# One step sequence for layer 0's row maxima, found half a pair ahead, with other slots for the third steps

## The chip, the cores and the metric

The kernel runs on one core of a Trainium2 chip. The metric is the device time of one execution in microseconds (us), smaller is better. Before the change it is 1639.65 us, the median of three executions (1639.27 to 1640.0 us). The engines are TensorE (PE in the profile), VectorE (DVE), ScalarE (ACT), GpSimd (POOL) and SyncE (SP), which issues the loads. Each runs its own list of instructions in order and waits for the others by semaphores.

## The reference, cut to what matters

The program is a two-layer decoder over 1024 tokens of width 128 and a context of 6404 rows of width 96. The change touches the cross attention of layer 0, and what is laid beside its last part. The cross attention has 8 heads of 64, which the kernel works in 4 pairs:

```python
q = (x @ Wq).reshape(B, Nq, HEADS, DIM_HEAD)
k = (context @ Wk).reshape(B, context.shape[1], HEADS, DIM_HEAD)
v = (context @ Wv).reshape(B, context.shape[1], HEADS, DIM_HEAD)
sim = jnp.einsum('bihd,bjhd->bhij', q, k) * SCALE
attn = jax.nn.softmax(sim, axis=-1)
out = jnp.einsum('bhij,bjhd->bihd', attn, v)
```

The softmax needs a shift near each row's largest score. Layer 1 later rounds the context to integers (`jnp.round(x / i_scale)`), projects it, and needs the largest magnitudes for the scales; the kernel begins that in the last pair of layer 0.

## The kernel before

A pair of heads is worked in two halves of 512 queries (`hf` counts them, 0 to 7). In a half the 51 key tiles of 128 rows go by in 26 units of two tiles, and each unit is a *slot*: 52 slots for each pair, `s` from 0 to 51. Nothing is scheduled at run time. Each engine has the same loop over pairs and slots, and the lists written out in `ITEMS` and the step tables say what stands in each slot.

In a slot TensorE computes the scores of the unit's two tiles (L2153, 6 pairs of matmuls), and the values of the unit before (L2167, 4 pairs, fp32). The two heads lie on 64 rows each, so two matmuls run side by side. ScalarE takes the exponential of each tile (L933), 128x1024. VectorE (L1432) adds three quarters of it to a running sum, and GpSimd (L708) the last quarter (`dve_part`, `SHARE`), in halves 0 to 5. In halves 6 and 7 VectorE adds all.

The row maxima are found ahead, from rounded keys and queries. The keys are folded: max(a, b) = (a + b)/2 + |a - b|/2, so the kernel makes sums and differences of keys half a context apart (`k16_in`, L2004 and L2005, called `kd` and `ks` in the tables; `k16_out` copies them to `K16`). A *step* is one tile of 128 queries of one head against one chunk of 512 differences and 512 sums: TensorE writes the difference scores into bank 6 (`x_ps`) and the sum scores of the step before into bank 7 (`y_ps`), both L2199; ScalarE writes the magnitude of bank 6 to `MC` (L959, `x_cp`); VectorE combines bank 7 with it and takes the maximum (`half_max`, L1382, `mx`). Step m on TensorE waits for ScalarE's step m-1 and VectorE's step m-2. The last chunk has 130 columns only, and takes up to three query tiles in a step.

Before the change pair 0's maxima, for all 1024 queries, are found ahead of the loop by themselves (`max_alone` over the 52 items of `ALONE0`, L2116, L912, L1382, chunks of twice the width). The maxima of pair p+1 are found inside pair p: 102 steps (`STEPS`, `NM`) in its slots 2 to 50, two in a slot, and a third one in slots 32, 36, 40, 44 and 48 (`THIRD_M`). In slots with a third step it lies between the score matmuls of the first and the second tile (`split_steps`). At the pair's end VectorE turns the maxima into shifts (`shifts`) and writes them on diagonals (`diagonals`), which `seeds` adds to the scores by matmuls (L2138).

Bank 5 of the PSUM serves one after the other: next pair's queries (`q`), keys (`dk`, fp32-like from three products, in the odd slots from 27), values (`v`, in the even slots from 28), denominators (`den`), output projection (`wo`). In pair 3 there are no steps, and the `CHAIN` list of layer 1 lies beside the slots: `scale`, `round` (VectorE L1570, then ScalarE L985), `project` (TensorE into banks 6 and 7, from slot 12), `max`. GpSimd finds the maximum over partitions (L716).

Of the kernel before, what the change touches and what calls it, by code (L numbers as in the profile page):

```python
# [99 lines left out]
def micro_steps(s):  # L100
    if not FIRST_M <= s <= LAST_M:
        return []
    a = 2 * (s - FIRST_M) + sum(t < s for t in THIRD_M)
    return list(range(a, a + 2 + (s in THIRD_M)))


assert micro_steps(LAST_M)[-1] == NM


def split_steps(s):  # L110
    steps = micro_steps(s)
    return steps[0:1], steps[1:-1], steps[-1:]
# [44 lines left out]
BANK_OF = {("q", 0): 6, ("q", 1): 7, ("kd", 0): 6, ("ks", 0): 7}  # L159


def bank_of(x):
    return BANK_OF.get((x[0], x[1][1]), 5) if x[0] in ("q", "kd", "ks") else 5


BANK5 = [x for p in range(PAIRS) for s in range(SLOTS) for x in ITEMS[p][s] if x[0] in FREED_BY and bank_of(x) == 5]
# [2545 lines left out]
```

## Time and profile before

| | |
|---|---|
| median of 3 executions | 1639.65 us |
| profiled execution, its own time | 1638.51 us |
| span of the profiled execution | 1636.8 us |
| TensorE busy | 1530.1 us (93% of the span) |
| VectorE busy | 1286.3 us (79%) |
| ScalarE busy | 1126.0 us (69%) |
| GpSimd busy | 490.9 us (30%) |
| granted TensorE clock, mean | 0.964 |

The busy time of an engine is the time in which at least one of its instructions shows as running. Instructions of an engine overlap at their ends, so the pace of an engine is better read from the starts of consecutive instructions than from their durations. The maxima by themselves take the span from 59.6 to about 125 us, the four pairs follow from 128.6 to about 1000 us, and 636.8 us of other work follow.

### The profile page before, as it was taken

What the parts mean: (1) busy time and instruction counts of PE and PEld (TensorE: products, weight loads), DVE (VectorE), ACT (ScalarE), POOL (GpSimd) and SP (SyncE); (2) the same over time, 40 slices, a digit from 0 to 9 for tenths busy, and PEclk for the clock granted to TensorE, in tenths of its full rate; (3) what the DMA queues carried; (4) which work ended last, traced back from release to release, by engine and by line L of the source; (5) the groups of instructions that cost most, each with busy time, mean ns of one, the idle gap of its engine ahead of it and who ended that gap; (6) DMA issues with size and microseconds to landing.
All of it is one profiled execution on the core that took longest, in us unless ns stands there. A gap on an engine that the chain in (4) does not pass through costs nothing.

```text
span 1636.8 us, 27033 instructions
## 1 busy us (share of the span) xinstructions
PE 1530.1 (93%) x9058; PEld 548.9 (34%) x9058; DVE 1286.3 (79%) x2319; ACT 1126.0 (69%) x1541; POOL 490.9 (30%) x488
## 2 busy tenths in 40 slices
PE   6889999999999999999999998899997979999986
PEld 4312333333333333333333223344444612222223
DVE  6898987879977779878789897877775666787766
ACT  6787777768877778777777786655554469676643
POOL 6303343334543334433300010345451012233100
PEclk9759999999999999999999998999999979999998
DMA  4000000000200000000010000111100000000000
GB/s 135 7 1 11 1 1 1 1 2 11 54 1 2 1 1 1 3 1 11 20 32 3 1 1 19 37 46 45 45 27 1 1 1 2 0 1 1 1 14 13
DMA packets 14834, 22.79 MB, mean 14 GB/s; under 512 B 1990, under 2 KB 11766, under 8 KB 14710
## 3 DMA queue, kind: packets, MB, share of 16 engines
q1 hardware_dynamic: 14710, 21.22, 4.6%
q8 instruction: 68, 1.11, 0.3%
q14 instruction: 56, 0.46, 0.1%
HBM read 20.69 MB, written 0.52 MB: 13 GB/s over the span
## 4 chain that ended last, share of the span: by engine, by line
PE 69%; issue 11%; DVE 9%; POOL 5%; ACT 4%; DMA 0%; POOLq 0%; SPq 0%; DVEq 0%; ACTq 0%
PE PS L2167 22%; PE PS L2153 15%; PE PS L2511 6%; PE PS L2199 5%; POOL WRK L734 5%; PE PS L2498 3%; DVE KNB L1382 3%; PE PS L2020 2%; PE PS L2012 2%; PE PS L2116 2%; PE PS L2540 2%; PE PS L2450 1%; PE PS L2435 1%; PE PS L2004 1%; ACT KNB L959 1%
## 5 line engine op out<-in xcount | busy, mean ns | idle before, releaser
L1382 DVE CUSTOM_DVE_ANT_0 KNB<-PS,KNB 128x512 f16<-128x512 f32 (+2 forms) x500 | 338.5, 690 | 152.4 <-PE PS L2199 106.9
L1432 DVE TENSOR_TENSOR WRK<-WRK 128x768 f32<-128x768 f32 (+3 forms) x400 | 425.2, 1063 | 15.3 <-ACT WRK L933 8.4
L933 ACT ACTIVATE WRK<-PS 128x1024 f32<-128x1024 f32 (+1 forms) x408 | 401.4, 1022 | 47.6 <-PE PS L2153 39.2
L2167 PE MATMUL PS<-WRK,V 128*64 128x512 f32 (+1 forms) x1632 | 395.7, 605 | 0.0
L708 POOL TENSOR_TENSOR WRK<-WRK 128x256 f32<-128x256 f32 x300 | 274.7, 916 | 395.6 <-ACT WRK L933 394.6
L959 ACT ACTIVATE KNB<-PS 128x512 f16<-128x512 f32 (+2 forms) x306 | 180.9, 591 | 77.8 <-PE PS L2199 77.2
L2344 PE MATMUL PS<-WRK,KNB 128*128 128x512 f16 x828 | 188.3, 381 | 7.1 <-POOL WRK L734 2.7
L2167 PEld LDWEIGHTS PS<-WRK,V 128*64 128x64 f32 (+1 forms) x1632 | 99.3, 136 | 192.7 <-issue 154.5
L2153 PE MATMUL PS<-KNB,KB 64*128 64x512 f16 (+1 forms) x1224 | 156.5, 377 | 0.0
L2153 PE MATMUL PS<-Q,KB 64*128 64x512 f16 (+1 forms) x1224 | 153.0, 377 | 0.0
L1162 ACT ACTIVATE WRK<-PS 128x1024 f32<-128x1024 f32 x100 | 102.4, 1024 | 51.1 <-PE PS L2498 47.6
L734 POOL TENSOR_TENSOR WRK<-KB,WRK 128x1024 f16<-128x1024 f32 x46 | 98.4, 2140 | 119.5 <-ACT WRK L1088 119.5
L2344 PEld LDWEIGHTS PS<-WRK,KNB 128*128 128x128 f16 x828 | 80.8, 98 | 106.7 <-issue 4.3
L1846 DVE TENSOR_TENSOR WRK<-WRK 128x768 f32<-128x768 f32 (+2 forms) x100 | 103.8, 1038 | 10.6 <-ACT WRK L1162 8.9
L2511 PE MATMUL PS<-WRK,V 128*64 128x512 f32 (+1 forms) x408 | 112.0, 617 | 0.0
L1624 DVE TENSOR_TENSOR KA<-PS,KB 128x1024 f32<-128x1024 f32 x46 | 56.3, 1225 | 48.3 <-PE PS L2344 48.3
L757 POOL TENSOR_TENSOR WRK<-WRK 128x256 f32<-128x256 f32 x72 | 56.2, 781 | 126.5 <-ACT WRK L1162 126.5
L2199 PE MATMUL PS<-KNB,Q 64*128 64x512 f16 (+1 forms) x448 | 79.3, 357 | 9.4 <-DVE MXP L1382 5.2
L2153 PEld LDWEIGHTS PS<-Q,KB 64*128 64x128 f16 (+1 forms) x1224 | 55.6, 94 | 88.8 <-ACT WRK L933 20.5
L2153 PEld LDWEIGHTS PS<-KNB,KB 64*128 64x128 f16 (+1 forms) x1224 | 59.6, 94 | 62.6 <-issue 12.7
L912 ACT ACTIVATE KNB<-PS 128x1024 f16<-128x1024 f32 x60 | 61.2, 1023 | 17.3 <-DVE MXP L1382 10.0
L1075 ACT ACTIVATE KB<-PS 128x1024 f32<-128x1024 f32 x46 | 47.1, 1023 | 35.0 <-PE PS L2344 35.0
(379 smaller groups left out, 1834.2 us busy)
## 6 DMA issues: line engine op xcount, KB each, us to landing
V<-in_moe_w_dram SPq DMA_DIRECT2D x44, 192.0 KB, 2.4
KNB<-in_ctx_fm_dram SPq DMA_DIRECT2D x6, 384.0 KB, 8.4
X<-in_ctx_fm_dram SPq DMA_DIRECT2D x12, 192.0 KB, 2.4
...
```

The costliest lines, as they stand in the source:

```text
L708: e.tensor_tensor(total, total, part, ALU.add).then_inc(S("acc_pool"), 1)
L734: e.tensor_tensor(H_LO[hslot], MH[hslot % 2], H_HI[hslot], ALU.subtract).then_inc(S("h_lo"), 1)
L933: e.activation(PR[0:r, u % 2, b, :], bank(2 * b, 2 * b + 2, slice(0, r)), ACT.Exp).then_inc(S("exp"), 1)
L959: e.activation(MC[:, m % 2, 0:w], PS[:, 6, 0:w], ACT.Abs).then_inc(S("x_cp"), 1)
L1382: return e.tensor_tensor_reduce(diffs, sums, diffs, 0.5, NEG, ALU.add, ALU.max, accum_out=out)
L1432: e.tensor_tensor(total, total, part, ALU.add).then_inc(S("acc"), 1)
L1846: e.tensor_tensor(total, total, part, ALU.add).then_inc(S("acc"), 1)
L2153: ins = e.matmul(PS[0:r, 2 * b + h, :], keys[rows, j * P:j * P + r], queries[rows, :], start=False, stop=(k == 2), skip_group_check=True)
L2167: ins = e.matmul(PS[h * HD:(h + 1) * HD, 4, :], V[0:r, j, h * HD:(h + 1) * HD], PR[0:r, unit_no(hf, i) % 2, b, h * HALF:(h + 1) * HALF], s ...
L2199: ins = e.matmul(PS[:, b, k * w:(k + 1) * w], QH[(p + 1) % 2][rows, t * P:(t + 1) * P], K16[rows, off + a:off + a + w], start=True, stop=True)
L2344: ins = e.matmul(bank(b + h), w_[:, part, :], rows[:, h * HALF:(h + 1) * HALF], start=start and i == 0, stop=stop and i == 2, skip_group_c ...
L2511: ins = e.matmul(PS[g * HD:(g + 1) * HD, 4, :], V2[n // 2][0:w, j, :], PR1[t % len(PR1)][0:w, g * HALF:(g + 1) * HALF], start=(i == 0), st ...
```

## The change

1. `ALONE0` has 26 items in place of 52: only the first 512 queries of pair 0 ahead of the loop.
2. `STEPS` becomes two lists of 52 steps, one for each half of queries, and all later halves (1 to 7) form one sequence of `NSTEP` = 364 steps that runs through the slots from slot 0 of pair 0 on: two in every slot, pairs' ends included, until slot 11 of pair 3.
3. Third steps: in pair 0 in slots 3, 4, 5, 23, 24, 26, 36, 40, 44, 48; in pairs 1 and 2 in slots 6, 9, 14, 16, 17, 20, 21, 23, 24, 26; none in pair 3. So 30 where there were 15.
4. `shifts` and its diagonals now come for one half at a time, seven times, at the start of the slot behind the one in which a half's last step lies: slots 25 and 49 of pair 0, 20 and 44 of pair 1, 16 and 39 of pair 2, and 12 of pair 3.
5. The sums and differences of the next pair's keys move to slots 6/7, 9/10, 13/14, 16/17, 20/21, 23/24 and 25/26. The queries move to slots 1 and 2. All of them use bank 5; before, the queries and the first chunk used banks 6 and 7, in slots 0 and 1.
6. GpSimd takes its quarter of the sums in half 6 too (`POOL_HALVES` = 7), and its three maxima over partitions lie between those sums.
7. The rounded context goes to `KA[1]` instead of `KN[0]`.

```diff
-STEPS = full_then_rest(NFULL, lambda t: (0, 1), 3)
-NM = len(STEPS)
+TILES_H = NT // 2
+STEPS = [[(c, [t], g) for c in range(NFULL) for t in range(TILES_H * u, TILES_H * u + TILES_H) for g in range(2)]
+         + [(NFULL, list(range(TILES_H * u + a, TILES_H * u + b)), g) for a, b in ((0, 3), (3, TILES_H)) for g in range(2)] for u in range(2)]
+NM = len(STEPS[0])
...
-ALONE0 = full_then_rest(NDC - 1, lambda t: (0, 1), 6)
+ALONE0 = [(d, [t], g) for d in range(NDC - 1) for t in range(TILES_H) for g in range(2)] + [(NDC - 1, [0, 1, 2, 3], g)
...
+POOL_HALVES = 2 * PAIRS - 1
...
-    return SHARE if hf < 2 * (PAIRS - 1) else T
+    return SHARE if hf < POOL_HALVES else T
...
-THIRD_M = (32, 36, 40, 44, 48)
...
+NSTEP = NM * (2 * PAIRS - 1)
+WITH_KEYS = (6, 9, 14, 16, 17, 20, 21, 23, 24, 26)
+THIRD_M = [(3, 4, 5, 23, 24, 26, 36, 40, 44, 48)] + [WITH_KEYS] * (PAIRS - 2) + [()]
+
+
+def first_step(p, s):
+    return min(2 * (p * SLOTS + s) + sum(len(x) for x in THIRD_M[:p]) + sum(t < s for t in THIRD_M[p]), NSTEP + 1)
...
+def split_steps(p, s):
+    steps = micro_steps(p, s)
+    return steps[:1], steps[1:-1], steps[1:][-1:]
...
+K16_AT = (6, 9, 13, 16, 20, 23, 25)
...
-        at[0] += [("wk", n), ("q", (n, 0)), ("q", (n, 1))]
-        at[1] += [("wv", n), ("kd", (n, 0)), ("ks", (n, 0))]
-        for c in range(1, NMC):
-            at[4 + 3 * c].append(("kd", (n, c)))
-            at[5 + 3 * c].append(("ks", (n, c)))
+        at[0].append(("wk", n))
+        at[1] += [("wv", n), ("q", (n, 0))]
+        at[2].append(("q", (n, 1)))
+        for c, k in enumerate(K16_AT):
+            at[k].append(("kd", (n, c)))
+            at[k + 1].append(("ks", (n, c)))
...
-        EMB = [KN[0].bitcast(BF16), KN[1].bitcast(BF16), KN[0].bitcast(BF16)]
+        EMB = [KA[1][:, :].bitcast(BF16), KN[1].bitcast(BF16), KN[0].bitcast(BF16)]
...
-                    if s == SLOTS - 1 and p + 1 < PAIRS:
-                        shifts(micro_base(p + 1), NMC, 2 * NT)
-                        e.wait_ge(S("sc"), tile_no(2 * p, 0, 0) + 1)
-                        diagonals(0, 2, NT)
+                    first, mid, last = split_steps(p, s)
+                    if ready(p, s):
+                        shifts(ready(p, s), STEP0 + ready(p, s) * NM, NMC)
```

How the order of instructions changes is shown at three places. The first is TensorE in pair 1, slots 13 (from its values on) and 14, to the first matmuls of slot 15. L2199 and L2224 are a step's matmuls, L2153 and L2177 the scores, L2004/L2005 and L2028/L2029 the sums and differences of keys, L2167 and L2191 the values. Before:

```order
L2167 MATMUL PS<-WRK,V 64x512 x4
L2199 MATMUL PS<-KNB 128x512 x2
L2153 MATMUL PS<-Q,KB 128x512 x12
L2199 MATMUL PS<-KNB 128x512 x2
L2004 MATMUL PS<-CTX,WK 128x512
L2005 MATMUL PS<-CTX,WK 128x512
L2167 MATMUL PS<-WRK,V 64x512 x4
L2199 MATMUL PS<-KNB 128x512 x2
```

The same place after:

```order
L2191 MATMUL PS<-WRK,V 64x512 x4
L2224 MATMUL PS<-KNB,Q 128x512 x2
L2177 MATMUL PS<-Q,KB 128x512 x6
L2224 MATMUL PS<-KNB,Q 128x512 x2
L2177 MATMUL PS<-Q,KB 128x512 x6
L2224 MATMUL PS<-KNB,Q 128x512 x2
L2028 MATMUL PS<-CTX,WK 128x512
L2029 MATMUL PS<-CTX,WK 128x512
L2191 MATMUL PS<-WRK,V 64x512 x4
L2224 MATMUL PS<-KNB,Q 128x512 x2
```

The slot has a third step between the two sixes of scores; the key matmuls stay behind the last step.

The second place is VectorE in pair 0, slots 48 and 49. L1382 and L1413 are the maxima (each with a short read of its result), L1432 and L1461 the sums, L1281 and L1312 the low parts of keys. After:

```order
L1461 TENSOR_TENSOR WRK<-WRK 128x768
L1413 ISA KNB,MXP<-PS,KNB 128x130
L1413 ISA MXP 128x1
L1312 TENSOR_TENSOR KB<-PS,KB 128x512
L1435 TENSOR_REDUCE NEGM<-MXP 128x8
L1440 TENSOR_TENSOR DIAG<-ident,NEGM 128x512 x2
L1461 TENSOR_TENSOR WRK<-WRK 128x768
L1413 ISA KNB,MXP<-PS,KNB 128x512
L1413 ISA MXP 128x1
```

Before, the shifts lie at the pair's end, in slot 51, where the steps have ended:

```order
L1382 ISA KNB,MXP<-PS,KNB 128x130
L1382 ISA MXP 128x1
L1403 TENSOR_REDUCE NEGM<-MXP 128x16
L1409 TENSOR_TENSOR DIAG<-ident,NEGM 128x512 x2
L1432 TENSOR_TENSOR WRK<-WRK 128x768 x2
L1281 TENSOR_TENSOR KB<-PS,KB 128x260
L1409 TENSOR_TENSOR DIAG<-ident,NEGM 128x512 x2
L1432 TENSOR_TENSOR WRK<-WRK 4x768
```

The reduction and its two diagonal instructions have moved ahead of a sum and of the next slot's maxima.

The third place is ScalarE in pair 3, from slot 5 on. L933 and L964 are exponentials, L985 and L1016 the rounding, L989 the magnitudes of a step. Before:

```order
L933 ACTIVATE WRK<-PS 128x1024 x4
L985 ACTIVATE KNB<-CTX,NMAG 96x1024
L933 ACTIVATE WRK<-PS 128x1024 x2
L985 ACTIVATE KNB<-CTX,NMAG 96x1024
L933 ACTIVATE WRK<-PS 128x1024 x2
```

After:

```order
L1016 ACTIVATE KA<-CTX,NMAG 96x1024
L989 ACTIVATE KNB<-PS 128x512
L964 ACTIVATE WRK<-PS 128x1024 x2
L989 ACTIVATE KNB<-PS 128x512
L1016 ACTIVATE KA<-CTX,NMAG 96x1024
L989 ACTIVATE KNB<-PS 128x512
```

Two magnitudes now stand in each slot beside two exponentials and a rounding.

## Rows read from the trace of the kernel before

**Rows 1.** Windows by stage: busy us (and instructions) of each engine, clock, DMA share.
```profile
59.60:128.60 69.00, 53.88 (x228) 10.13 (x228) 63.38 (x133) 52.82 (x55) 0.00 (x0) 0.51 0.00 1
...
822.50:1000.00 177.50, 177.50 (x1076) 54.65 (x1075) 157.75 (x165) 139.59 (x156) 8.13 (x12) 1.00 0.02 4
```

**Rows 2.** Timeline, VectorE at the maxima by themselves: start, us, what, idle before.
```profile
98.82 1.23 DVE L1382 CUSTOM_DVE_ANT_0 KNB<-PS,KNB 128x1024 f16<-128x1024 f32 x1
...
103.81 1.23 DVE L1382 CUSTOM_DVE_ANT_0 KNB<-PS,KNB 128x1024 f16<-128x1024 f32 x1
...
121.33 0.29 DVE L1382 CUSTOM_DVE_ANT_0 KNB<-PS,KNB 128x130 f16<-128x130 f32 x1
...
125.39 2.50 DVE L1409 TENSOR_TENSOR DIAG<-ident,NEGM 128x512 f16<-128x512 f16 x4
```

**Rows 3.** Timeline, TensorE in pair 2: slots 5 and 10.
```profile
612.99 0.39 PE L2199 MATMUL PS<-KNB,Q 64*128 64x512 f16 x2
...
616.69 0.39 PE L2199 MATMUL PS<-KNB,Q 64*128 64x512 f16 x2
...
632.74 0.39 PE L2199 MATMUL PS<-KNB,Q 64*128 64x512 f16 x2
...
634.27 0.38 PE L2199 MATMUL PS<-KNB,Q 64*128 64x512 f16 x2
...
636.98 0.39 PE L2199 MATMUL PS<-KNB,Q 64*128 64x512 f16 x2
```

**Rows 4.** Timeline, TensorE in pair 0: slots 30 and 32.
```profile
254.20 0.39 PE L2199 MATMUL PS<-KNB,Q 64*128 64x512 f16 x2
...
258.68 0.39 PE L2199 MATMUL PS<-KNB,Q 64*128 64x512 f16 x2
...
263.43 0.39 PE L2199 MATMUL PS<-KNB,Q 64*128 64x512 f16 x2
...
264.72 0.39 PE L2199 MATMUL PS<-KNB,Q 64*128 64x512 f16 x2 [0.25 <-DVE MXP L1382]
...
266.47 0.39 PE L2199 MATMUL PS<-KNB,Q 64*128 64x512 f16 x2
...
268.66 0.39 PE L2199 MATMUL PS<-KNB,Q 64*128 64x512 f16 x2
```

**Rows 5.** Timeline, VectorE and ScalarE in slot 32 of pair 0.
```profile
265.42 0.59 ACT L959 ACTIVATE KNB<-PS 128x512 f16<-128x512 f32 x1
...
264.49 0.95 DVE L1432 TENSOR_TENSOR WRK<-WRK 128x768 f32<-128x768 f32 x1
265.36 0.68 DVE L1382 CUSTOM_DVE_ANT_0 KNB<-PS,KNB 128x512 f16<-128x512 f32 x1
265.97 0.08 DVE L1382 DVE_READ_ACCUMULATOR2_ANT MXP<- 128x1 f32 x1
```

**Rows 6.** Windows: slots 0 to 2 of pair 2.
```profile
591.20:605.00 13.80, 13.55 (x81) 4.95 (x82) 8.08 (x12) 10.28 (x18) 4.67 (x6) 1.00 0.00 1
```

**Rows 7.** Groups by form, pair 3, slots 4 to 11: busy, mean ns, idle before.
```profile
L933 ACT ACTIVATE WRK<-PS 128x1024 f32<-128x1024 f32 x16 | 15.5, 1022 | 4.8 <-PE PS L2153 4.8
...
L985 ACT ACTIVATE KNB<-CTX,NMAG 96x1024 bf16<-96x1024 f32 x6 | 6.9, 1143 | 0.0
L1570 DVE TENSOR_SCALAR CTX<-CTX,AI 96x1024 f32<-96x1024 f32 x6 | 4.2, 698 | 0.0
...
L1447 DVE RECIPROCAL QS<-QS 128x128 f32<-128x128 f32 x4 | 3.8, 946 | 0.0
```

**Rows 8.** Windows: slots 4 to 11 of pair 3.
```profile
836.30:862.50 26.20, 26.20 (x164) 7.97 (x164) 24.46 (x27) 22.07 (x23) 0.00 (x0) 1.00 0.00 1
```

**Rows 9.** Groups by form, VectorE, pairs 0 to 2.
```profile
L1432 DVE TENSOR_TENSOR WRK<-WRK 128x768 f32<-128x768 f32 x294 | 296.5, 1008 | 1.5 <-DVE WRK L1428 0.5
...
L1409 DVE TENSOR_TENSOR DIAG<-ident,NEGM 128x512 f16<-128x512 f16 x12 | 9.9, 868 | 0.1
```

**Rows 10.** The page's costliest groups: GpSimd's sums.
```profile
L708 POOL TENSOR_TENSOR WRK<-WRK 128x256 f32<-128x256 f32 x300 | 274.7, 916 | 395.6 <-ACT WRK L933 394.6
```

More of the change, by code:

```diff
@@ L93, in rows_of, with micro_steps, half_step, step @@
     return P if j < KT - 1 else TAIL
-THIRD_M = (32, 36, 40, 44, 48)
[L100 to L112, printed above, removed]
+NSTEP = NM * (2 * PAIRS - 1)
[3 more added lines that the diff above has]
+    return min(2 * (p * SLOTS + s) + sum(len(x) for x in THIRD_M[:p]) + sum(t < s for t in THIRD_M[p]), NSTEP + 1)
+def micro_steps(p, s):
+    return list(range(first_step(p, s), first_step(*divmod(p * SLOTS + s + 1, SLOTS))
+                      if p * SLOTS + s + 1 < PAIRS * SLOTS else NSTEP + 1))
+def half_step(m):
+    return 1 + m // NM, m % NM
+def step(m):
+    h, k = half_step(m)
+    return STEPS[h % 2][k]
+def half_done(p, s):
+    done = [m // NM for m in micro_steps(p, s) if m and m % NM == 0]
+    return done[0] if done else None
+def ready(p, s):
+    return half_done(*divmod(p * SLOTS + s - 1, SLOTS)) if p * SLOTS + s else None
+def split_steps(p, s):
+    steps = micro_steps(p, s)
+    return steps[:1], steps[1:-1], steps[1:][-1:]
 def inside(x):
     return x[0] == "dk"
-def micro_base(p):
-    return len(ALONE0) + NM * p
+STEP0 = len(ALONE0)
+K16_AT = (6, 9, 13, 16, 20, 23, 25)
 def items_of(p):
@@ L158 @@
             "bits": "bit_dve"}
[L159 to L166, printed above, removed]
+BANK5 = [x for p in range(PAIRS) for s in range(SLOTS) for x in ITEMS[p][s] if x[0] in FREED_BY]
+for _p in range(PAIRS - 1):
+    for _c, _k in enumerate(K16_AT):
+        _steps = [m for m in range(NSTEP) if step(m)[0] == _c]
+        _last = max(m for m in _steps if half_step(m)[0] == 2 * _p + 1)
+        _first = min(m for m in _steps if half_step(m)[0] == 2 * _p + 2)
+        assert first_step(_p, _k) > _last + 1 and first_step(*divmod(_p * SLOTS + _k + 2, SLOTS)) <= _first
 def freed(x):
@@ L713, in _ @@
                         add_up(hf, i, b)
-            for i in range(3):
-                e.wait_ge(S("ax"), i + 1)
-                e.partition_all_reduce(AM[:, i:i + 1], AX[:, i:i + 1], P, RED.max).then_inc(S("am"), 1)
+                    if hf == POOL_HALVES - 1 and i == CHAIN.index(("max", 1)) - 1:
+                        largest(1)
+            largest(2)
             link(e.memset(SWAP, 0.0))
@@ L1005, in _ @@
                     hf, i = 2 * p + s // NU, s % NU
-                    first, mid, last = split_steps(s) if p + 1 < PAIRS else ([], [], [])
-                    magnitude(p, first)
+                    first, mid, last = split_steps(p, s)
+                    magnitude(first)
                     exp(hf, i, 0)
-                    magnitude(p, mid)
+                    magnitude(mid)
                     for x in filter(inside, ITEMS[p][s]):
@@ L1013, in _ @@
                         exp(hf, i, 1)
-                    magnitude(p, last)
+                    magnitude(last)
                     if i == 0 and hf:
@@ L1414, in _ @@
             max_alone(0, ALONE0, True)
-            shifts(len(ALONE0), NDC, 2 * NT)
-            for u in range(2):
-                diagonals(u, 2, NT)
+            shifts(0, STEP0, NDC)
             def add_up(hf, i, b):
@@ L2265, in _ @@
                     hf, i = 2 * p + s // NU, s % NU
-                    first, mid, last = split_steps(s) if p + 1 < PAIRS else ([], [], [])
+                    first, mid, last = split_steps(p, s)
                     if i == 0:
```

114 lines of the change are left out of this document (57 added, 57 removed).

## The prediction

> **What bounds the kernel now.** I read the windows by stage first, then the timeline of each stage, by the starts of instructions. The maxima by themselves are a stage of VectorE: TensorE sits idle for 15 of the 69.0 us of its window, at the low one of its clock levels (0.51 of 2.4 GHz), and VectorE is busy for 63.4 [rows 1]. Its maxima start 4.99 us apart for four items, so an item takes 1.247 us [rows 2]. In pair 3 TensorE is busy all 177.5 us of its window [rows 1]. In the slots of pairs 0 to 2 TensorE sets the pace too: a plain slot with two steps takes 3.70 us from first step to first step, one with a key sum or difference 4.24 [rows 3], one with values of the next pair 4.48 [rows 4]. Pair 3 has no steps, and its slots 4 to 11 take 26.2 us, 3.275 each [rows 8]. A step is thus cheap when it stands in pairs: (3.70 - 3.275)/2 = 0.21 us.
>
> Third steps aren't cheap. Slot 32 has three steps and values: from its first step at 263.43 to the next slot's at 268.66 are 5.23 us, against 4.48 for slot 30, which does the same with two [rows 4]. The third costs 0.75, of which 0.21 is work. The rest is waiting: the first step starts at 263.43, the second at 264.72, with 0.25 us idle until VectorE's maximum, 1.29 us apart [rows 4]. With two steps they stand 1.53 apart, filled with all 12 score matmuls [rows 3]; with three only 6 of these lie between. The second step's maximum runs from 265.36, behind a sum that starts at 264.49, and its result is read at 265.97 to 266.05; ScalarE's magnitude ends at 266.01 [rows 5]. So the third step can't start before about 266.20, 2.77 behind the first. Here it starts at 266.47, since the value matmuls (12 of them, ahead of the last step in such a slot) fill that time [rows 4].
>
> **The change, part by part.**
>
> *Ahead of the loop.* 24 large items go: 24 x 1.247 = 29.9 us. Of 16 small maxima, which run from 121.33 to the shifts just ahead of 125.39 (3.8 us for 16 of them), 8 go: 1.9 us [rows 2]. Gain 31.8. Four diagonal instructions (2.50 us for four) become two, but TensorE needed only the first two, so nothing.
>
> *Third steps.* Of before's 15, three in each pair (slots 32, 36, 40) cost 0.75. Slot 44 and slot 48 I take at 1.0 and 0.7 (estimates around the same row, the latter with narrow steps). Together 3 x (2.25 + 1.7) = 11.9 us. Of the new 30, 23 stand in slots where nothing lies between the second and the third step but 6 score matmuls: slots 3, 4, 5, 23, 24 of pair 0 and nine in each of pairs 1 and 2. The keys made in these slots don't fill the gap, since the order puts them behind the last step. There the last step starts 2.77 behind the first instead of 1.53 [rows 3 to 5], and all behind it is TensorE's own work: 1.25 us each, 28.8. Three in slot 26 cost 0.75 each (that slot has one tile of values only, and ScalarE paces it: one more magnitude and a small key copy), 2.2. Four remain with values in pair 0: 3.3. Sum 34.3, so net +22.4. Bounds: from below 0.21 of pure work each, which gives 30 x 0.21 = 6.3 and net -5.6; from above 1.5, net about +28. I take 1.25, because both waits are read from a slot of the same kind.
>
> *Two steps where there were none.* Slots 0 to 2 take 13.80 us with two query products, both first keys and two steps [rows 6]. Afterwards: 3.6 (two steps, values), about 5.2 (ScalarE has the attention copy, two weight copies and values behind it) and 4.6, 13.4; the moved keys cost 2 x 0.54 (4.24 - 3.70, [rows 3]) later. In slots 49 to 51 two full steps stand for narrow ones or none: about 1.1 for each pair. Narrow steps now end each of seven halves: 0.4 saved each. Pair 0's first slots +0.5. Net 3 x (-0.4 + 1.1 + 1.1) + 0.5 - 2.8 = about +3.
>
> *Shifts.* Reduction and two diagonals take some 1.9 us (0.87 each, [rows 9], and a short reduction), seven times instead of four, and they stand ahead of a sum and the next maximum. VectorE has 0.7 us to spare in a plain slot; what is over, about 1.1 us, delays the second step. In slots 16 and 20, with three steps, that is all seen (1.1 each), in 25, 44 and 39 about 0.9, 0.9 and 0.2, in 49 0.2, in 12 none: +4.4. Bounds 0 and 8.
>
> *Pair 3.* Slots 0 to 11 get 22.5 steps. In slots 0 to 3: two steps at 0.21 each and a little for ScalarE's copies, +1.8. In slots 4 to 11 other engines become the pace. ScalarE: two exponentials (1.02), two magnitudes (0.6), one rounding (1.14) [rows 5, 7] are 4.4 by durations, some 3.85 by starts (0.1 overlap each). VectorE: two sums at 0.87 and two maxima at 0.61 by starts [rows 5], one scaling at 0.65, is 3.6, and 4.5 in the four slots with a reciprocal (0.95, [rows 7]). So about 3.85 in four, 4.45 in four, less in the last: 32.9 against 26.2 [rows 8], +6.7. Sum +8.5. Bounds: work alone 22.5 x 0.21 = 4.7, and 14 when reciprocal, scaling and steps wait for each other in turn.
>
> *GpSimd's quarter in half 6.* This is counted above: VectorE's sum takes 1.01 instead of 1.22 us. Its quarter on GpSimd takes 0.92 [rows 10], two in 3.7 us, so GpSimd keeps up. All else in half 6 is TensorE's pace, so no gain. One rule speaks against this part. The trace shows VectorE's 294 sums at 1.008 us beside GpSimd's [rows 9], where an undisturbed one takes 0.95 [rows 5]: 0.06 of disturbance. The Trainium skill (SBUF — State Buffer, "SBUF: two separate sides") says that VectorE with two SBUF inputs and GpSimd exclude each other from a shared port pair for a whole instruction. Taken to the full, each of the 14 sums in slots 5 to 11 would wait 0.92 more. By the rows it's 14 x 0.06 = 0.8, by the rule 13 us. I go by the rows, and keep the other as a rival.
>
> **Sum.** -31.8 + 22.4 + 3 + 4.4 + 8.5 = +6.5 us. The profiled execution took 1638.51, so 1645.0 by its own time; the median of the runs shown is 1.1 above it, so I say 1646.
>
> **Rivals.**
> 1. *Third steps are cheaper than read*, which ends on the other side. If ScalarE and VectorE, with more time in these longer slots, have the second step's results early (the maximum ahead of the sum's end, for instance), the 23 thirds cost 0.75 as in slot 32, not 1.25: -11.5 us, 1634.5. At pure work they'd cost 0.21 and the time would be 1622. Against it: VectorE's order has the sum between the two maxima, whatever the load. It decides where a third step costs under 0.83 us: 23 x 0.42 = 9.6 less than forecast is 1636.4, which is 0.2% under the median. Chance 0.25.
> 2. *The sums exclude each other.* If each of the 14 sums of slots 5 to 11 waits for a whole GpSimd sum, that is 14 x 0.92 = 13 us [rows 10], of which 3 may lie in VectorE's spare time: +10 to +13, 1656 to 1659. VectorE would then be the pace of slots 4 to 11. The rows say 0.06 per sum. Chance 0.08.
> 3. *Shifts and pair 3 are hidden.* The shifts fall into VectorE's spare time and the steps of pair 3 cost their work: -4.4 - 3.8, 1638, no change. For it: three-step slots leave VectorE over a microsecond idle. Chance 0.17.
> 4. *Forecast*, chance 0.50, 1640 to 1654 by itself.
>
> **How the numbers follow.** Most likely 1646. The range goes from 1633 (rival 1 with its half microsecond) to 1656 (rival 2's lower end), with about 0.1 left out on each side. A measurement here tells 0.2% (3.3 us) from no change. Faster: rival 1, and a bit of rival 3, 0.27. Same: most of rival 3 and the forecast's lower end, 0.19. Slower: 0.54.
>
> **What would show it.** In the profile after, the first scores should start some 32 us earlier than 128.6. In slots 9, 14, 16, 17, 20, 21 of pairs 1 and 2 the first step to the next slot's first step should be about 5.5 us, with idle time of TensorE ahead of second and third step released by VectorE's maxima (L1413 there), 0.4 and 0.6 us. In slots 16 and 20 the shifts add one more. Pair 3's slots 4 to 11 should take 33 us, with TensorE's busy share falling below all of it. Slots 27 to 51 of pairs 1 and 2 should take less than before, by about 3 us. The prediction is wrong if the three-step slots take under 5.0 us, or if slots without third steps wait on ScalarE or VectorE through the pairs.

## The result, and the profile after

| | before | after |
|---|---|---|
| median | 1639.46 us (1638.01 to 1640.0, 4 executions) | 1667.98 us (1666.37 to 1670.74, 4 executions) |
| profiled execution | 1638.51 us | 1666.37 us |
| first scores | 128.6 us | 97.0 us |
| first scores to the last of the loop | 871.5 us | 928.1 us |
| behind the loop | 636.7 us | 639.6 us |

The changed kernel takes 1.0177 times as long (95% interval 1.0159 to 1.0195). It is slower, which was forecast with 0.54, but by 28.5 us where the forecast had 6.5, and the time lies outside the range of 1633 to 1656. The work ahead of the loop shrank as forecast (31.6 us, forecast 31.8). The loop grew by 56.6 us where the terms sum to 38.3. The stages as windows of the changed kernel (busy us of PE, PEld, DVE, ACT and POOL with their instructions, clock, DMA share, GB/s), against [rows 1] and [rows 8]:

```profile
59.60:97.00 37.40, 27.51 (x118) 5.34 (x120) 32.10 (x68) 25.78 (x28) 0.00 (x0) 0.54 0.00 0
...
828.50:1025.10 196.60, 184.23 (x1128) 58.58 (x1128) 167.94 (x221) 150.08 (x178) 57.41 (x63) 0.98 0.01 4
...
847.50:878.60 31.10, 29.37 (x199) 10.52 (x197) 30.95 (x67) 28.34 (x37) 16.81 (x16) 1.00 0.01 2
828.50:847.50 19.00, 15.68 (x109) 5.50 (x107) 12.39 (x26) 13.29 (x20) 6.01 (x9) 1.00 0.10 27
915.80:938.00 22.20, 15.19 (x82) 4.24 (x80) 12.00 (x13) 7.98 (x8) 12.13 (x12) 0.85 0.00 1
```

Pair 3 is the place to look at. Before, TensorE was busy in all of its 177.5 us [rows 1]. Now it is idle for 12.4 of 196.6, and not in the slots where the steps lie (847.5 to 878.6, 1.7 us idle) but in two short stretches: 3.3 of the 19.0 us that begin the pair, and 7.0 of the 22.2 us behind 915.8, where half 6 has no step left. Slots 2, 22 and 23 take 7.07, 10.35 and 5.01 us from first score matmul to first score matmul; before, each took 3.27. Half 6 of before is 90.5 us long, that of after 109.5.

What these slots wait for, from the timeline of all engines behind slot 22's stall (start, us, engine, what, idle before and its releaser):

```profile
925.06 1.94 ACT L964 ACTIVATE WRK<-PS 128x1024 f32<-128x1024 f32 x2 [9.73 <-POOL WRK L733]
926.11 1.38 DVE L1461 TENSOR_TENSOR WRK<-WRK 128x768 f32<-128x768 f32 x1 [9.65 <-ACT WRK L964]
...
926.14 1.89 PE L2177 MATMUL PS<-Q,KB 64*128 64x512 f16 x8 [7.01 <-ACT WRK L964]
```

Read it from the bottom: TensorE's scores wait for a bank that ScalarE has to empty, ScalarE's exponential waits 9.73 us for a buffer that GpSimd must have added up, and VectorE waits for that exponential. Not all of the loss is idle time. Slot 23, behind the stall, has no idle time of TensorE, and still takes 5.01 us in place of 3.27: the granted clock is at its low level (1.2 GHz) for a part of it (window as above).

```profile
926.10:931.10 5.00, 4.96 (x20) 1.30 (x20) 4.71 (x7) 2.94 (x3) 4.43 (x5) 0.63 0.01 3
```

Its 12 score matmuls take 2.74 us and its 8 value matmuls 2.41, where 1.47 and 1.94 are usual (slot 24). That is the whole 1.74 us of slot 23, so of the 12.2 us that slots 2, 22 and 23 lose, some 10.4 are idle time and 1.7 are the clock after it.

GpSimd's own timeline around both stalls (L733 are its quarters of the sums, L738 the maximum over partitions, L729 the first quarter of a half):

```profile
825.91 0.72 POOL L733 TENSOR_TENSOR WRK<-WRK 4x256 f32<-4x256 f32 x1 [2.43 <-ACT WRK L964]
832.49 0.38 POOL L738 PARTITION_ALL_REDUCE AM<-AX  x1 [5.86 <-issue]
832.75 0.46 POOL L729 COPY WRK<-WRK 128x256 f32<-128x256 f32 x1
840.26 4.17 POOL L733 TENSOR_TENSOR WRK<-WRK 128x256 f32<-128x256 f32 x5 [7.06 <-issue]
...
908.87 1.21 POOL L733 TENSOR_TENSOR WRK<-WRK 128x256 f32<-128x256 f32 x1 [0.19 <-ACT WRK L964]
916.67 0.38 POOL L738 PARTITION_ALL_REDUCE AM<-AX  x1 [6.59 <-issue]
924.23 3.84 POOL L733 TENSOR_TENSOR WRK<-WRK 128x256 f32<-128x256 f32 x4 [7.18 <-issue]
```

The maximum itself shows as 0.38 us. Ahead of it GpSimd stands still for 5.86 and 6.59 us, behind it for 7.06 and 7.18 us before the next sum, and the profile names no releaser ("issue"). From the last sum before the maximum to the next one behind it are some 14 us, four slots, in which the exponentials' buffers run out. The trace of before has the first of these gaps already:

```profile
820.45 0.81 POOL L708 TENSOR_TENSOR WRK<-WRK 4x256 f32<-4x256 f32 x1 [2.25 <-ACT WRK L933]
827.06 0.38 POOL L716 PARTITION_ALL_REDUCE AM<-AX  x1 [5.80 <-issue]
```

There it cost nothing, since GpSimd had no sums in half 6. It is the row that the prediction left out. The Trainium skill (GPSIMD Engine Reference, "2.1 Instruction dispatch") says that the first call of a freshly loaded GpSimd kernel pays a code load of about 6 us with no instruction of its own in the profile. The gaps ahead of the maxima agree in size (5.80 to 6.59); that they are such loads no run here shows. What the trace does show is where each gap begins. Two entries MODIFY_POOL_CONFIG of GpSimd's own queue stand about 0.2 us behind the last sum, and two more behind the maximum, ahead of the next sum (source views of L738 and L733, window 905 to 930):

```profile
L738 POOLq MODIFY_POOL_CONFIG  x2: 8/8/8, 910.3 to 910.3; - x2
L733 POOLq MODIFY_POOL_CONFIG  x2: 82/82/83, 917.0 to 917.0; - x2
```

The changed kernel has 20 of them, the kernel before 12. Ahead of its third maximum the changed kernel has two as well, at 937.6 us, but this maximum has to wait for VectorE's value until 989.0 and starts 0.14 us behind it: there the gap lies inside a wait and costs nothing.

In pairs 0 to 2 the third steps cost what was forecast. TensorE in slot 16 of pair 2 (timeline), which stands beside slots 5 and 10 of [rows 3]:

```profile
656.42 0.39 PE L2224 MATMUL PS<-KNB,Q 64*128 64x512 f16 x2
656.65 0.81 PE L2177 MATMUL PS<-KNB,KB 64*128 64x512 f16 x6
657.72 0.39 PE L2224 MATMUL PS<-KNB,Q 64*128 64x512 f16 x2 [0.27 <-DVE MXP L1413]
657.94 0.82 PE L2177 MATMUL PS<-KNB,KB 64*128 64x512 f16 x6
659.20 0.39 PE L2224 MATMUL PS<-KNB,Q 64*128 64x512 f16 x2 [0.44 <-DVE MXP L1413]
...
661.93 0.39 PE L2224 MATMUL PS<-KNB,Q 64*128 64x512 f16 x2
```

The last step starts 2.78 us behind the first (forecast 2.77), after two waits for VectorE's maxima of 0.27 and 0.44 us (0.4 and 0.6 were forecast), and the slot takes 5.51 us, 1.27 more than with two steps. And the rule that VectorE and GpSimd exclude each other, from the groups by form of slots 4 to 11 of pair 3 (busy, mean ns of one, idle before):

```profile
L733 POOL TENSOR_TENSOR WRK<-WRK 128x256 f32<-128x256 f32 x16 | 17.5, 1093 | 15.1 <-ACT WRK L964 14.5
L964 ACT ACTIVATE WRK<-PS 128x1024 f32<-128x1024 f32 x16 | 15.5, 1023 | 1.2 <-PE PS L2177 1.0
...
L1461 DVE TENSOR_TENSOR WRK<-WRK 128x768 f32<-128x768 f32 x16 | 15.1, 945 | 0.0
```

VectorE's sums take 945 ns in these slots, as an undisturbed one in [rows 5], and it is GpSimd whose sums have grown, to a mean of 1093 ns from 916 in [rows 10]. Behind slot 11 it is otherwise. VectorE's sums there (878.6 to 937 us, by form):

```profile
L1461 DVE TENSOR_TENSOR WRK<-WRK 128x768 f32<-128x768 f32 x28 | 32.9, 1177 | 12.8 <-ACT WRK L964 10.9 <-DVE WRK L1461 0.5
```

So VectorE's sums are disturbed in half 6, but no slot's time shows it: slots 12 to 21 take what they took before, to within 0.1 us.

### The profile page after: what moved, and what is told of

Read it like the earlier page. It is cut to its first block, busy times and chain, and to the rows that moved or that the text cites. A ratio compares the mean times of both kernels' runs of the same rounds, so it can differ in the third digit from the quotient of the medians.

```text
span 1664.6 us, 27396 instructions
## 1 busy us (share of the span) xinstructions
PE 1528.5 (92%) x9041; PEld 554.0 (33%) x9058; DVE 1283.7 (77%) x2371; ACT 1126.5 (68%) x1573; POOL 531.4 (32%) x539
## 3 DMA queue, kind: packets, MB, share of 16 engines
q8 instruction: 68, 1.11, 0.3%
## 4 chain that ended last, share of the span: by engine, by line
PE 66%; issue 13%; DVE 10%; ACT 5%; POOL 5%; DMA 0%; POOLq 0%; DVEq 0%; SPq 0%; ACTq 0%
PE PS L2191 21%; PE PS L2177 13%; PE PS L2224 6%; PE PS L2537 6%; POOL WRK L766 5%; PE PS L2524 3%; DVE KNB L1413 2%; PE PS L2044 2%; DVE WRK L1461 2%; PE PS L2036 2%; PE PS L2566 2%; ACT KNB L989 1%; PE PS L2140 1%; PE PS L2018 1%; PE PS L2476 1%
## 5 line engine op out<-in xcount | busy, mean ns | idle before, releaser
L1413 DVE CUSTOM_DVE_ANT_0 KNB<-PS,KNB 128x512 f16<-128x512 f32 (+2 forms) x524 | 343.1, 664 | 181.4 <-PE PS L2224 137.6
L733 POOL TENSOR_TENSOR WRK<-WRK 128x256 f32<-128x256 f32 x350 | 314.3, 898 | 486.9 <-ACT WRK L964 468.2
L1461 DVE TENSOR_TENSOR WRK<-WRK 128x768 f32<-128x768 f32 (+3 forms) x400 | 419.4, 1048 | 18.7 <-ACT WRK L964 13.9
L964 ACT ACTIVATE WRK<-PS 128x1024 f32<-128x1024 f32 (+1 forms) x408 | 403.2, 1022 | 41.9 <-PE PS L2177 20.2
L2191 PE MATMUL PS<-WRK,V 128*64 128x512 f32 (+1 forms) x1632 | 396.1, 605 | 0.0
L989 ACT ACTIVATE KNB<-PS 128x512 f16<-128x512 f32 (+2 forms) x364 | 212.2, 583 | 118.4 <-PE PS L2224 118.0
L2191 PEld LDWEIGHTS PS<-WRK,V 128*64 128x64 f32 (+1 forms) x1632 | 99.3, 136 | 195.9 <-issue 158.1
L2177 PE MATMUL PS<-Q,KB 64*128 64x512 f16 (+1 forms) x1224 | 155.4, 379 | 7.0 <-ACT WRK L964 7.0
L2177 PE MATMUL PS<-KNB,KB 64*128 64x512 f16 (+1 forms) x1224 | 159.6, 378 | 0.0
L1193 ACT ACTIVATE WRK<-PS 128x1024 f32<-128x1024 f32 x100 | 102.3, 1023 | 51.3 <-PE PS L2524 47.9
L2224 PE MATMUL PS<-KNB,Q 64*128 64x512 f16 (+1 forms) x448 | 80.4, 358 | 24.0 <-DVE MXP L1413 16.5
L789 POOL TENSOR_TENSOR WRK<-WRK 128x256 f32<-128x256 f32 x72 | 56.2, 781 | 126.7 <-ACT WRK L1193 126.7
L2177 PEld LDWEIGHTS PS<-Q,KB 64*128 64x128 f16 (+1 forms) x1224 | 58.8, 94 | 86.6 <-ACT WRK L964 23.9
L2177 PEld LDWEIGHTS PS<-KNB,KB 64*128 64x128 f16 (+1 forms) x1224 | 61.4, 94 | 59.3 <-issue 12.4
L2224 PE MATMUL PS<-KNB 64*128 64x512 f16 (+1 forms) x336 | 61.3, 360 | 16.2 <-DVE MXP L1413 12.5
```

The costliest lines, as they stand in the source:

```text
L733: e.tensor_tensor(total, total, part, ALU.add).then_inc(S("acc_pool"), 1)
L964: e.activation(PR[0:r, u % 2, b, :], bank(2 * b, 2 * b + 2, slice(0, r)), ACT.Exp).then_inc(S("exp"), 1)
L989: e.activation(MC[:, m % 2, 0:w], PS[:, 6, 0:w], ACT.Abs).then_inc(S("x_cp"), 1)
L1413: return e.tensor_tensor_reduce(diffs, sums, diffs, 0.5, NEG, ALU.add, ALU.max, accum_out=out)
L1461: e.tensor_tensor(total, total, part, ALU.add).then_inc(S("acc"), 1)
L2177: ins = e.matmul(PS[0:r, 2 * b + h, :], keys[rows, j * P:j * P + r], queries[rows, :], start=False, stop=(k == 2), skip_group_check=True)
```

## Experiments

"Loop" is the time from the first score matmul to the end of the last one in the profiled execution, in which a single slot's time repeats from kernel to kernel to within some 0.02 us where nothing is changed. The median moves by more than the loop does, since the part behind the loop varies by itself (below). Line numbers differ a little from kernel to kernel.

**Run 1: e1_pool6.** The changed kernel, with GpSimd's sums only in halves 0 to 5 and the maxima over partitions behind them.

```diff
-POOL_HALVES = 2 * PAIRS - 1
+POOL_HALVES = 2 * PAIRS - 2
...
-                if hf == POOL_HALVES - 1:
-                    largest(0)
...
+            for i in range(3):
+                largest(i)
```

> The changed kernel, with GpSimd's quarter of the sums and its three maxima over partitions put back as before (sums in halves 0 to 5 only, all three maxima behind them). All else as changed. Theory A (GpSimd is away for about 14 us each time a maximum over partitions stands between its sums, and the exponentials wait for it): slot 2 of pair 3 falls from 7.1 to 3.7 us, slots 22 and 23 from 15.4 to 6.5, 12 us in all. VectorE's sums in half 6 take 1.22 instead of 0.95 us again, which costs up to 4 us in slots 4 to 11. So 1656 to 1660 us. Theory B (the sums of VectorE and GpSimd disturb each other in half 6) expects a gain too, but spread over slots 4 to 11, and slots 2, 22 and 23 as they are.

1656.54 us (1654.78 to 1662.85), 1.0117 times before (1.0094 to 1.0140): 11.4 us less than the changed kernel. Slots 2, 22 and 23 of pair 3 fell by 3.37, 7.08 and 1.74 us, 12.2 in all; slots 5 to 10 of that pair grew by 2.6, since VectorE adds all four quarters there. GpSimd's maxima in this kernel:

```profile
833.49 0.38 POOL L738 PARTITION_ALL_REDUCE AM<-AX  x1 [5.93 <-issue]
910.82 0.35 POOL L738 PARTITION_ALL_REDUCE AM<-AX  x1 [76.96 <-DVE AX L1584]
980.49 0.35 POOL L738 PARTITION_ALL_REDUCE AM<-AX  x1 [69.32 <-DVE AX L1584]
```

Only the first has the idle time without a releaser. The second and third, with nothing of another kind between them, start when VectorE's maximum is there, and MODIFY_POOL_CONFIG stands ahead of the first alone. So it is the alternation with the sums that costs, not the operation.

**Run 2: e2_copy.** The changed kernel, GpSimd's sums of half 6 kept, and the first two maxima over partitions replaced by a copy on GpSimd. It leaves out the largest value over the partitions for the scales of the first two roundings, so each partition is scaled by its own.

```diff
+                if i < 2:
+                    e.tensor_copy(AM[:, i:i + 1], AX[:, i:i + 1]).then_inc(S("am"), 1)
+                    return
                 e.partition_all_reduce(AM[:, i:i + 1], AX[:, i:i + 1], P, RED.max).then_inc(S("am"), 1)
```

> The changed kernel, with GpSimd's quarter in half 6 kept, and the first two maxima over partitions replaced by plain copies on the same engine at the same places. It leaves out the maximum over partitions for the scales of the first two roundings. Theory A: the 12 us of slots 2, 22 and 23 go, and slots 4 to 11 stay: 1656 us. Theory B: nothing goes, 1668 us, since all sums stay where they are.

1654.26 us (1653.46 to 1654.46), 1.0089 (1.0072 to 1.0106). The same three slots fell by the same 3.37, 7.08 and 1.74 us and no other moved by more than 0.1: loop 917.4 where the changed kernel has 928.1. That is 10.7 less and not 12.2, since slot 1 of pair 0 took 6.41 us here and 4.89 there. It takes one or the other in every kernel that has the steps in that slot, 6.4 where a second stretch at the low clock follows the first (about 102 to 106 us), and 4.9 where the clock stays high from 100 us on. GpSimd's timeline at the two places:

```profile
826.38 0.71 POOL L733 TENSOR_TENSOR WRK<-WRK 4x256 f32<-4x256 f32 x1 [2.44 <-ACT WRK L967]
827.05 0.97 POOL L739 COPY AM<-AX 128x1 f32<-128x1 f32 x1
830.94 0.40 POOL L729 COPY WRK<-WRK 128x256 f32<-128x256 f32 x1 [2.92 <-ACT WRK L967]
...
908.12 0.19 POOL L739 COPY AM<-AX 128x1 f32<-128x1 f32 x1 [0.95 <-DVE AX L1590]
908.31 2.91 POOL L733 TENSOR_TENSOR WRK<-WRK 128x256 f32<-128x256 f32 x2
```

With the sums and their position unchanged, the gaps are gone with the operation. The quarter of the sums in half 6 costs nothing by itself, and is worth the 2.6 us that run 1 lost.

**Run 3: e3_fill.** The changed kernel, where in slots with three steps the key matmuls lie ahead of the last step.

```diff
-                        if x[0] == "v" and mid:
+                        if x[0] in ("v", "kd", "ks") and mid:
                             bank5(x)
```

> The changed kernel, with the key matmuls of a slot that has a third step put ahead of its last step instead of behind it. The theory of the prediction (the last step waits 0.6 us for the second step's maximum and magnitude): the two key matmuls, 0.54 us, fit into that wait, so each of the 20 slots with third step and full keys apart from slot 26 falls from 5.5 to 5.0 us: 10.8 us, 1657. Rival (the wait is not there, or the key copy on ScalarE delays the last magnitude as much): 1668 us.

1657.87 us (1652.28 to 1662.64), 1.0107 (1.0078 to 1.0136). Of the 20 slots with keys and three steps 19 fell by 0.50 to 0.54 us; slot 14 of pair 2 fell by 0.25, and the one behind it grew by as much. Slot 16 of pair 2 now:

```profile
652.44 0.82 PE L2177 MATMUL PS<-KNB,KB 64*128 64x512 f16 x6
653.20 0.39 PE L2028 MATMUL PS<-CTX,WK 96*128 96x512 f16 x1
653.42 0.38 PE L2029 MATMUL PS<-CTX,WK 96*128 96x512 f16 x1
653.74 0.39 PE L2224 MATMUL PS<-KNB,Q 64*128 64x512 f16 x2
```

The second wait of 0.44 us is filled by the keys' 0.54. What a third step costs is a gap that this slot's other work can fill, if it stands ahead of it. The loop is only 5.1 us shorter, because other slots grew: slot 1 of pair 0 by 1.53, as in run 2, and slot 3 of pair 3 by 2.68. GpSimd's stall in slot 2 is the same as in the changed kernel (3.25 us of TensorE idle in place of 3.32); what differs is the clock after it. Slot 3, the same 32 matmuls, here and in the changed kernel:

```profile
834.30:841.60 7.30, 7.30 (x32) 2.21 (x30) 4.08 (x9) 3.73 (x5) 2.69 (x4) 0.62 0.00 0
```

```profile
842.90:847.50 4.60, 4.60 (x32) 1.58 (x30) 4.29 (x9) 3.52 (x5) 3.09 (x4) 1.00 0.00 0
```

So the clock can take another 2.7 us behind such a stall, in some executions and not in others.

**Run 4: e4_thirds.** The kernel before, with only its third steps moved to slots with keys.

```diff
-THIRD_M = (32, 36, 40, 44, 48)
+THIRD_M = (7, 10, 13, 16, 19)
```

> The kernel before, with only its third steps moved from slots 32, 36, 40, 44, 48 (with values) to 7, 10, 13, 16, 19 (with keys), in pairs 0 to 2. The prediction's price: 15 x 1.25 = 18.8 us come and 11.9 go, +6.9, 1646 us. Rival (a third step costs 0.75 us wherever it stands): 1640 us or a little less.

1649.65 us (1647.49 to 1650.65), 1.0061 (1.0044 to 1.0077). Each moved step costs 1.27 or 1.28 us in pairs 1 and 2, up to 1.98 in pair 0, and the slots that lost theirs fell by 0.75 (32, 36, 40), 0.97 (44) and 0.75 (48). The loop grew by 8.7. The price does not come from the longer sequence: it is that of the slot.

**Run 5: e5_keyslots.** The kernel before, with its third steps in the odd slots where products of the next pair's keys are made (`dk`, three matmuls).

```diff
-THIRD_M = (32, 36, 40, 44, 48)
+THIRD_M = (31, 33, 37, 41, 47)
```

> The kernel before, with its third steps moved from the slots with values (32, 36, 40, 44, 48) to slots with full-precision keys (31, 33, 37, 41, 47). There three key matmuls already stand between the second and the third step, so only the first gap (0.43 us) is left to wait, and part of the 0.4 us for which such a slot waits today may lie in it: 0.25 to 0.65 us a third instead of 0.75 to 0.97. So 1631 to 1638 us. Rival: ScalarE, with two exponentials, three magnitudes and the key copy (3.8 us by starts, one behind the other), makes the third cost 0.75 or more: 1639 us or above.

1639.45 us (1637.57 to 1640.81), 0.9995 (0.9984 to 1.0007): no change in the median; in the profile the loop is 1.9 us shorter, the part behind it 2.7 and the part ahead of it 0.95 longer. A third step costs 0.66 us here (4.74 to 5.40 us; 0.56 in slot 47), at the upper end of what was expected, so the gain is at the lower end of the expected one and the median doesn't show it. The expectation missed. Slot 31 of pair 2:

```profile
721.28 0.39 PE L2199 MATMUL PS<-KNB,Q 64*128 64x512 f16 x2
721.51 0.81 PE L2153 MATMUL PS<-KNB,KB 64*128 64x512 f16 x6
722.59 0.39 PE L2199 MATMUL PS<-KNB,Q 64*128 64x512 f16 x2 [0.27 <-ACT KNB L959]
722.91 0.82 PE L2012 MATMUL PS<-KA,WK 96*128 96x512 f16 x3
```

Three matmuls lie behind the second step, so that the last one comes when VectorE's result is there. The wait that stays is the first one, 0.27 us.

**Run 6: e6_pool6_fill.** Runs 1 and 3 together.

```diff
-POOL_HALVES = 2 * PAIRS - 1
+POOL_HALVES = 2 * PAIRS - 2
...
-                        if x[0] == "v" and mid:
+                        if x[0] in ("v", "kd", "ks") and mid:
```

> The changed kernel, with GpSimd as before (first run of this study) and the key matmuls ahead of the last step (third run). If the two costs are separate, they add: 1656.5 - 10.4 = 1646 us. If they share a wait, over 1650.

1648.20 us (1645.75 to 1649.74), 1.0046 (1.0029 to 1.0062). The loop is 910.4 us, 17.7 less than the changed kernel's. Against run 1, which has the same clock in slot 1 of pair 0, it is 9.6 less, what the key slots fell by in run 3. The two causes add up.

**Run 7: e7_split.** Run 6, with the second diagonal instruction of `shifts` one slot later, for halves 2 and up.

```diff
-                for h in range(2):
+                for h in range(2) if half is None else (0,):
...
+                    if s and ready(p, s - 1) and ready(p, s - 1) > 1:
+                        second_diagonal(ready(p, s - 1))
```

> The same, with the second diagonal of six of the seven shifts put one slot later than the reduction and the first. The prediction's price of the shifts is 4.4 us in all, since 1.9 us stand in one piece where VectorE has 0.7 to spare. In two pieces of about 1 us most of it should go: 3 us less than the run before it. Rival: VectorE's backlog is carried over either way, no change.

1645.39 us (1643.71 to 1650.05), 1.0039 (1.0024 to 1.0053). The loop is shorter by 0.8 us only: four slots with shifts fell by 0.5 to 0.6, 2.3 in all, slot 20 of pair 1 behind one of them grew by 0.92, and slot 44 of pair 1, whose shifts had cost nothing, by 0.60. Two thirds of what the four gave back was moved, not hidden. The other 2 us of the median lie behind the loop.

**Run 8: e8_thirds_v.** Run 1, with the third steps of pairs 1 and 2 in ten of the slots that make the next pair's values.

```diff
-THIRD_M = [...] + [WITH_KEYS] * (PAIRS - 2) + [()]
+THIRD_M = [...] + [(30, 32, 34, 36, 38, 40, 42, 44, 48, 50)] * (PAIRS - 2) + [()]
```

> The changed kernel with GpSimd as before, and the third steps of pairs 1 and 2 in slots with values (30, 32, 34, 36, 38, 40, 42, 44, 48, 50) instead of those with sums and differences of keys. At 0.75 us instead of 1.27 each, and about 1.0 in slot 44: 9 us less than the first run of this study, 1647.5 us. Rival: in a row of such slots VectorE, which has the low parts of keys besides, falls behind and the thirds cost over 1 us: 1652 or above.

1646.12 us (1644.85 to 1648.76), 1.0045 (1.0033 to 1.0057). The loop is 10.0 us shorter than in run 1, of which 1.5 are in slot 1 of pair 0 (the clock, as in run 2); 8.5 are left for the third steps, where 9 were expected. Third steps cost 0.75 in plain value slots, and 0.98 to 2.28 where shifts or a normalization stand in the same slot.

**Run 9: e9_pool7_before.** The kernel before, with one part of the change alone: GpSimd's quarter in half 6, and its maxima between the sums.

```diff
-            for hf in range(2 * (PAIRS - 1)):
+            for hf in range(2 * PAIRS - 1):
+                if hf == 2 * PAIRS - 2:
+                    largest(0)
...
+                    if hf == 2 * PAIRS - 2 and i == 19:
+                        largest(1)
```

> The kernel before, with one part of the change alone: GpSimd also makes its quarter of the sums of half 6, with the maxima over partitions of the first two roundings between them. Theory A (GpSimd stands idle on both sides of each such maximum and falls behind): slots 2, 22 and 23 of pair 3 grow as they did in the changed kernel, where they stood +12.2 us over slots of 3.70 us; beside slots of 3.27 us, and less what DVE no longer has to add, +12 to +14 us in all, so about 1651 to 1654 us. Rival B (GpSimd's sums hold VectorE up): the cost lies spread over slots 3 to 25 of pair 3, by at most 25 x 0.06 = 1.5 us, and the time is within 2 us of 1639.5. Rival C (the wait comes of the whole half ahead, so not here, where third steps stand in half 6): no slot of pair 3 over 4.5 us but for those of steps.

1654.04 us (1653.54 to 1656.47), 1.0086 (1.0069 to 1.0102), 14.7 us over before. In the profile three slots of pair 3 account for it: slot 3 grew by 5.59, slot 22 by 7.20 and slot 23 by 1.33 us, and no other slot of pairs 0 to 3 but the very first by more than 0.12. The clock has a part in it here too (granted 0.82, 0.81 and 0.70 in the three). GpSimd:

```profile
828.01 0.38 POOL L713 PARTITION_ALL_REDUCE AM<-AX  x1 [5.93 <-issue]
828.27 0.46 POOL L704 COPY WRK<-WRK 128x256 f32<-128x256 f32 x1
835.86 7.85 POOL L708 TENSOR_TENSOR WRK<-WRK 128x256 f32<-128x256 f32 x7 [7.12 <-issue]
...
906.36 0.64 POOL L713 PARTITION_ALL_REDUCE AM<-AX  x1 [5.98 <-issue]
914.65 13.19 POOL L708 TENSOR_TENSOR WRK<-WRK 128x256 f32<-128x256 f32 x11 [7.64 <-issue]
```

This part alone brings half as much as the whole change, whether the steps are half a pair ahead or not. The stall hits slot 3 in place of slot 2, which the expectation had not foreseen; its size was foreseen.

**Run 10: e10_mixed.** Run 7, with the third steps of pairs 1 and 2 in slots 26, 29, 31, 33, 35, 37, 41, 45, 47 and 49.

```diff
-THIRD_M = [...] + [WITH_KEYS] * (PAIRS - 2) + [()]
+THIRD_M = [...] + [(26, 29, 31, 33, 35, 37, 41, 45, 47, 49)] * (PAIRS - 2) + [()]
```

> The kernel of e7 (the changed one without GpSimd's half 6, key matmuls ahead of the last step, diagonals apart), with the ten third steps of pairs 1 and 2 in slots 26, 29, 31, 33, 35, 37, 41, 45, 47 and 49 of each, in place of four in slots with three steps. Theory: a third step costs 0.64 to 0.75 us wherever its slot has filler, by runs e5 and e8, so the two pairs cost 20 x 0.7 less than in e7 for four-at-0.75 and six-at-1 each: 2 to 3 us less, about 1642 to 1643 us, still above the 1639.4 of before. Rival: the slots with the next pair's keys have no more room beside the shifts, and the time stays at 1645 or rises.

1641.02 us (1639.87 to 1643.06), 1.0010 (1.0001 to 1.0020). The loop is 5.0 us shorter than in run 7, of which 1.5 are in slot 1 of pair 0, the clock again; 3.5 come of the third steps, which cost 0.66 us in 14 of the 20 slots. The rival is out. The part of the expectation on what they cost in run 7 (four at 0.75, six at 1) was off: there they cost 0.6 to 1.1, slots 20 and 23 of pair 1 aside, where the shifts of one of the two kernels stand.

**Run 11: e11_pair0.** Run 10, with pair 0's third steps moved as well.

```diff
-THIRD_M = [(3, 4, 5, 23, 24, 26, 36, 40, 44, 48)] + ...
+THIRD_M = [(14, 16, 20, 26, 29, 31, 33, 35, 45, 47)] + ...
```

> The kernel of e10 with pair 0's ten third steps in slots 14, 16, 20, 26, 29, 31, 33, 35, 45 and 47 too. Theory (a third step costs what its slot can't fill): slots 3, 4, 5, 23 and 24 of pair 0 give back 1.27 each, or 1.0 to 1.3 in the two with keys, about 6.0 in all; slots 14, 16 and 20 take 0.76 each, and five of the next pair's key slots 0.66 each; those with values gave 0.75 to 0.97 each. Together 1.5 to 3 us less than e10's 1641.0, so 1638 to 1639.5, level with before (1639.3). Rival (the shifts and the first slots of pair 0 take it back, since VectorE must add the same): no change against e10, 1641.

1640.11 us (1637.07 to 1647.29), 1.0007 (0.9995 to 1.0020). The loop is 902.2 us, 2.4 less than in run 10, as the theory had it; slots 3, 4 and 5 are back at 3.70. The median shows 0.9 of it, within what the part behind the loop varies by. This is the best version with maxima half a pair ahead, and it is level with before, not better.

## Why the prediction was wrong

The sign held, the size didn't. The sign does not hang on the missed term: without GpSimd's 12.2 us and the 2.9 behind the loop the profiled execution would still be 12.8 us over the one before. By the prediction's own steps, in the profiled executions (27.9 us more than before, where the sum had 6.5):

| term | forecast | measured |
|---|---|---|
| ahead of the loop | -31.8 | -31.6 |
| pairs 0 to 2 (thirds, two steps, shifts) | +29.8 | +37.6 |
| steps in pair 3 | +8.5 | +6.7 |
| GpSimd's quarter in half 6 | 0 | +12.2 |
| behind the loop | 0 | +2.9 |

**The step that failed** is the sentence "two in 3.7 us, so GpSimd keeps up. All else in half 6 is TensorE's pace, so no gain." It priced the moved sums and not the instruction that the change puts between them. The change puts PARTITION_ALL_REDUCE between sums twice, with 13 and 14 us of GpSimd idle around it. The stalls cost 12.2 us over undisturbed slots (3.70 us for slot 2, 3.27 for 22 and 23), 1.7 of them by the low clock in slot 23. The sums by themselves did keep up, as run 2 shows, so that half of the sentence was right. Taking away either the sums (run 1) or the maximum (run 2) removed exactly the same 12.2 us, and adding both to the kernel before brought 14.1 us in three slots (run 9). That settles this cause. It also shows why the forecast's question about the two engines' ports was the wrong one: the weighed rule pointed at VectorE's sums. These stayed at 945 ns in slots 5 to 11, where the 13 us were priced, and where they grew, to 1177 ns behind slot 11, they cost no slot anything. Taken to the full on every sum, as the prediction did, the rule was also overpriced: in pairs 0 to 2 of the kernel before VectorE's sums take 1.11 us on average if they start while one of GpSimd's is running (107 of 294), and 0.95 if not. Rival 2 gave 1656 to 1659 for a slow half 6, nearer in time but by a mechanism that did not set the time.

**Third steps** were right: 1.27 in 1.25's place in slots with keys (run 4 the same), 0.75 with values, 0.65 in slot 26, and the removed ones came to 0.67 to 0.97. Rival 1, a cheaper third step, did not occur in the changed kernel; run 3 shows that it would by another order of the same instructions. Slots 6 and 9 of pairs 1 and 2 were 0.4 dearer (5.90 us), where a reciprocal or other work of VectorE's is near (that this is the reason was not tried); four slots, +1.6.

**The other small terms** of pairs 0 to 2 missed mostly in one direction. Slots 0 to 2 of the three pairs took 3.2 us more together, where the prediction's terms have -0.7, and 3.0 of that are in pair 0. The granted clock is part of it: the windows there show 0.85 in 128.6 to 132.5 before and 0.68 in 97.0 to 102.3 after. ScalarE's table load is another. Before, it stood ahead of the loop, at 124.47 us, where ScalarE had to wait anyway; now it stands in slot 0, behind a step's magnitude:

```profile
97.62 0.60 ACT L989 ACTIVATE KNB<-PS 128x512 f16<-128x512 f32 x1 [5.22 <-PE PS L2224]
98.23 1.28 ACT L964 ACT_TABLE_LOAD   x1
99.53 1.94 ACT L964 ACTIVATE WRK<-PS 128x1024 f32<-128x1024 f32 x2
101.35 0.60 ACT L989 ACTIVATE KNB<-PS 128x512 f16<-128x512 f32 x1
```

The next step on TensorE starts at 102.06, after 1.53 us idle for the magnitude at 101.35. How much each of the two is worth was not tried apart. The shifts measured about 5.1 in place of 4.4, but elsewhere than forecast: 1.5 us in slot 48 of pair 0 and in slot 38 of pair 2 (forecast 0.2 each), 1.5 in 19 and 20 of pair 1 (1.1), 0.4 in 24 and 25 of pair 0 (0.9), 0.1 in 15 of pair 2 (1.1), nothing in 44 (0.9). The narrow steps saved 0.2 to 0.4 us at a half's end, about a microsecond less in all than the 2.8 forecast, and slots 49 to 51 took 4.1 more together where 3.3 were forecast. With slots 6 and 9 these make 8.0 us over the forecast, where the table has 7.8; smaller ones of either sign are left.

**Pair 3's steps** came to 31.1 us in slots 4 to 11 (forecast 32.9), with slots at 3.70, 4.48 and 4.45 as worked out, but cheaper ones than 3.85 in the slots without a reciprocal. Slots 27 to 51 of pairs 1 and 2 fell by 2.7 and 1.4 (forecast about 3).

**Behind the loop** no instruction is changed that could take 2.9 us, and the difference comes and goes with the granted clock. A window in that part, before and after:

```profile
1021.00:1026.00 5.00, 4.80 (x16) 1.83 (x16) 3.12 (x9) 3.54 (x5) 0.00 (x0) 0.69 0.52 156
```

```profile
1046.00:1051.00 5.00, 4.22 (x10) 1.46 (x11) 3.89 (x10) 3.36 (x5) 0.00 (x0) 0.50 0.57 172
```

Over the profiled executions of all thirteen kernels, this part takes 636.6 to 637.0 us where the clock is at its low level (1.2 GHz) for 42 to 46 us of it, and 638.5 to 639.7 us where for 47 to 53 us. Kernels with the sequence of before stand in both groups, and so do those with the changed one. So it is a spread of some 3 us between executions, not a part of the change; that the clock is the whole of its cause was not tried. It is as large as 0.2% of the time, which is why the medians did not tell runs 5 and 11 from before, and run 10 only just.
